# Transposing attention probabilities by row halves, at another place in the order of the engines

## The reference

```python
xn = layernorm(x)                                  # x: 8 batches, 256 rows, 128 columns, float32
q  = rope(xn @ wq.T);  latent = xn @ w_kv_down.T   # 16 heads of 64; latent of 64
k  = rope(latent @ w_k_up.T);  v = latent @ w_v_up.T
s  = softmax(q @ k.T / 8 + causal) @ v @ wo.T      # per batch and head
g  = silu(2 * expert_of_each_row(xn))              # 8 experts, gelu, 128 -> 512 -> 128
out = x + s * g
```

## Time and profile before

| what | value |
|---|---|
| median of 3 runs | 302.62 us (302.54 to 303.06) |
| the profiled execution, its own time | 303.29 us |
| its span | 301.5 us |
| PE busy | 289.6 us (96%) |
| ACT, DVE, POOL busy | 239.3, 229.7, 213.5 us |
| granted TensorE clock | 1.0 of full speed throughout |

### The profile page before, as it was taken

The page is one execution under the profiler, slowest core; times in us unless marked ns, Lnnn a source line. Parts: engine busy times, 40 slices in busy tenths (PEclk is TensorE's granted clock), DMA queues, the critical chain, the costliest instruction groups (busy, mean ns, idle before and its releaser), DMA issues.

```text
span 301.5 us, 8603 instructions
## 1 busy us (share of the span) xinstructions
PE 289.6 (96%) x2362; PEld 235.0 (78%) x2362; DVE 229.7 (76%) x909; ACT 239.3 (79%) x863; POOL 213.5 (71%) x325
## 2 busy tenths in 40 slices
PE   8798999999999999999999989999999999999994
PEld 2576888888888888777776779999977778887663
DVE  4889998987777898988898723444377889898981
ACT  4278789898887889989998676677787898999971
POOL 2478878697778669999999982333226899998730
PEclk9999999999999999999999999999999999999999
DMA  6864685879333233444333382000234243543410
GB/s 192 249 133 115 114 276 148 205 194 300 87 75 68 60 75 83 107 101 102 90 97 90 112 245 55 2 0 2 66 93 108 64 113 99 121 106 109 113 37 17
DMA packets 39596, 33.35 MB, mean 111 GB/s; under 512 B 4801, under 2 KB 36674, under 8 KB 39554
## 3 DMA queue, kind: packets, MB, share of 16 engines
q1 hardware_dynamic: 38098, 30.51, 39.8%
q0 software_dynamic: 1024, 2.10, 2.4%
q10 hardware_dynamic: 432, 0.23, 0.3%
HBM read 11.07 MB, written 4.98 MB: 53 GB/s over the span
## 4 chain that ended last, share of the span: by engine, by line
PE 64%; POOL 14%; DVE 9%; issue 6%; DMA 3%; ACT 1%; POOLq 0%; SPq 0%; DVEq 0%; ACTq 0%
PE bank L1199 9%; PE bank L1187 9%; PE bank L1216 8%; PE bank L1450 7%; PE bank L1438 6%; PE bank L1233 6%; POOL probs L499 5%; POOL staged L488 5%; PE bank L1161 3%; DVE rot_out L617 3%; PE bank L1218 3%; PE bank L1189 3%; POOL xn L515 3%; DMA qk_sb<-staged 3%; DVE masked L633 2%
## 5 line engine op out<-in xcount | busy, mean ns | idle before, releaser
L975 ACT ACTIVATE pexp<-masked,negmax 128x128 f32<-128x128 f32 (+1 forms) x256 | 113.9, 452 | 2.2 <-DVE negmax L633 2.2
L499 POOL TENSOR_SCALAR probs<-pexp,rden 128x128 f32<-128x128 f32 (+1 forms) x195 | 84.3, 447 | 27.0 <-DVE rden L640 25.2
L633 DVE CUSTOM_DVE_ANT_0 masked<-bank,mask 128x128 f32<-128x128 f32 (+1 forms) x256 | 75.9, 352 | 21.4 <-PE bank L1189 20.5
L488 POOL TENSOR_TENSOR staged<-rot_out 128x512 f32<-128x512 f32 x56 | 71.4, 1278 | 16.2 <-DVE rot_out L617 15.6
L617 DVE TENSOR_TENSOR rot_out<-bank,rot 128x1024 f32<-128x1024 f32 x64 | 77.7, 1215 | 4.6 <-PE bank L1163 3.5
L997 ACT COPY probsT<-bank 128x384 f32<-128x384 f32 x126 | 54.0, 480 | 27.3 <-PE bank L1199 26.0
L1199 PE MATMUL bank<-ident,probs 128*128 128x128 f32 x384 | 54.0, 275 | 0.7 <-issue 0.5
L975 ACT ACTIVATION_READ_ACCUMULATOR pexp<-masked,negmax 128x1 f32 x256 | 50.0, 195 | 0.0
L1187 PE MATMUL bank<-qk_sb 64*128 64x256 f32 x256 | 47.0, 428 | 1.7 <-DMA qk_sb<-staged 1.3
L1199 PEld LDWEIGHTS bank<-ident,probs 128*128 128x128 f32 x384 | 43.0, 140 | 3.4 <-issue 1.2
L1233 PE MATMUL bank<-vo_sb,ctxT 128*128 128x128 f32 x256 | 37.8, 278 | 0.7 <-ACT ctxT L1004 0.7
(11 more groups left out here) (117 smaller groups left out, 483.6 us busy)
## 6 DMA issues: line engine op xcount, KB each, us to landing
qk_sb<-staged SPq DMA_DIRECT2D x128, 128.0 KB
w_sb<-in_w SPq DMA_DIRECT2D x2, 1024.0 KB, 5.8
w_sb<-in_w SPq DMA_DIRECT2D x4, 512.0 KB, 5.3
sorted_x<-z SPq DMA_DIRECT2D x1, 1408.0 KB, 8.0
sorted_g<-z SPq DMA_DIRECT2D x1, 1152.0 KB, 5.5
out<-res SPq DMA_DIRECT2D x8, 128.0 KB, 2.3
x_sb<-in_x SPq DMA_DIRECT2D x3, 256.0 KB, 3.8
rot<-in_c_rot SPq DMA_DIRECT2D x1, 512.0 KB, 5.7
```

The source lines that it names most:

```text
L488: pool.tensor_tensor(staged[:, n % 2, :, m % 2, :], rot_out[:, m % 2, :, 0:S], rot_out[:, m % 2, :, S:2 * S], op=ALU.add).then_inc(staged_ ...
L499: pool.tensor_scalar(probs[:, g % 2, i, c], pexp[:, g % 2, i, c], rden[:, g % 2, i, k:k + 1], 1.0, ALU.mult, ALU.mult).then_inc(probs_read ...
L633: t = dve.tensor_tensor_reduce(masked[:, g % 2, i, c], s_bank[i][:, c], mask[:, c], -1.0, -NEG * 1e8, ALU.add, ALU.min, negmax[:, g % 2, i ...
L975: e = act.activation(pexp[:, g % 2, i, c], masked[:, g % 2, i, c], ACT.Exp, bias=negmax[:, g % 2, i, k:k + 1], scale=-1.0, accum_out=rowsu ...
```

## The change

In slots 2 to 35 and in the periods (units 43 to 56), a transposition is made from 64 rows at a time: for each piece of 128 columns there are two transpositions, one of the upper 64 rows of `probs` into `bank2` and one of the lower 64 rows into `bank3`. A unit has 12 of them, of 64 rows by 128 columns, where it had six of 128 by 128. Each bank then holds both heads' halves, and ACT's two copies write runs of 64 columns; both copies wait for all 12.

The place moves too. `TURN_LAST` names the slots 2 to 35 and the odd units 43 to 55. There turn(g) is PE's last work of the slot or period, directly ahead of the next scores, and ACT's copies stand one slot later in its list, between the two exponentials of that slot. For the even units 44 to 56 turn(s) keeps its place behind scores(s+3). Since the copies of the odd unit now come later, values of two units in a period is cut into one call part for each unit, each with its own wait.

```diff
+TURN_LAST = (*range(2, G_LEAD - 4), *range(PERIODS[0] + 1, PERIODS[-1], 2))
+HALVED = (*TURN_LAST, *PERIODS[1:])
...
+        def turned_half(g, i):
+
+            whole = probsT[:, g % 4].rearrange("p i (k q c) -> p (i k) q c", q=2, c=HD)
+            return whole[:, :, i, :]
...
+                if g in HALVED:
+                    act.wait_ge(probsT_done, 2 * g + 2)
+                    for i in range(2):
+                        act.copy(turned_half(g, i), t_bank[i][:, 0:SW].rearrange("p (n c) -> p n c", c=HD)
+                                 ).then_inc(probsT_ready, 1)
+                    return
...
+                if g - 1 in TURN_LAST:
+                    turned_probs(g - 1)
                 if more:
                     exponentials(g + 1, 1)
...
-                if g not in (G_LEAD, G_LEAD + 1, LATE):
+                if g not in (G_LEAD, G_LEAD + 1, LATE) and g not in TURN_LAST:
                     turned_probs(g)
...
             def turn(g):
 
+                if g in HALVED:
+                    wait(pe, probsT_ready, 2 * g)
+                    for i in range(2):
+                        for k in range(3):
+                            if k < 2:
+                                pe.wait_ge(probs_ready[i][k], g + 1)
+                            for o, r in zip(t_bank, half_rows):
+                                t = pe.transpose(o[:, (3 * i + k) * HD:(3 * i + k + 1) * HD],
+                                                 probs[r, g % 2, i, k * P:(k + 1) * P], ident[r, r])
+                        t.then_inc(probsT_done, 1)
+                    return
...
-                pe.wait_ge(probsT_ready, 2 * (g + n))
-                pairs = slice(g % 4, g % 4 + n)
...
+                parts = ((g, 1), (g + 1, 1)) if g in PERIODS and g + 1 in TURN_LAST else ((g, n),)
+                for j, k in parts:
+                    pe.wait_ge(probsT_ready, 2 * (j + k))
...
             # period(s)
-                turn(s + 1)
+                if s + 1 not in TURN_LAST:
+                    turn(s + 1)
                 for m in items(s + 1):
                     project(m)
                 for m in items(s)[1:]:
                     project(m)
+                if s + 1 in TURN_LAST:
+                    turn(s + 1)
...
             # slot(g)
-                else:
+                elif g not in TURN_LAST:
                     turn(g)
...
+                if g in TURN_LAST:
+                    turn(g)
                 for m in items(g)[1:]:
                     project(m)
```

More of the change, by code:

```diff
@@ L1211, in values @@
                     wait(pe, ctx_ready, values_through(min(g, LATE)) - 1)
-                pe.wait_ge(probsT_ready, 2 * (g + n))
-                pairs = slice(g % 4, g % 4 + n)
[L1214 to L1218, removed]
+                parts = ((g, 1), (g + 1, 1)) if g in PERIODS and g + 1 in TURN_LAST else ((g, n),)
+                for j, k in parts:
+                    pe.wait_ge(probsT_ready, 2 * (j + k))
+                    pairs = slice(j % 4, j % 4 + k)
+                    at = slice((j - g) * S, (j - g + k) * S)
+                    o = (w_bank if g == LATE else o_bank)[:, at].rearrange("p (n s) -> p n s", s=S)
+                    for i, r in enumerate(half_rows):
+                        pe.matmul(o[r, :, :], lat_all[:, 2 * b, :], probsT[:, pairs, i, 0:S], start=True, stop=False)
+                    for i, r in enumerate(half_rows):
+                        m = pe.matmul(o[r, :, P:S], lat_all[:, 2 * b + 1, :], probsT[:, pairs, i, S:SW],
+                                      start=False, stop=True)
                 m.then_inc(pv_done, 1)
```

## The result

The changed kernel takes 305.27 us (median of 7 runs, 304.05 to 306.26), the kernel before 303.05 on the same chip: ratio 1.0074, 95% interval 1.0052 to 1.0095. It is 0.7% slower, where 301.5 and a gain were forecast. The profiled execution took 305.54 us with a span of 303.1.

What follows compares the result with a forecast made beforehand. PE was taken as the bound, with DVE or POOL also full in some slots and a loop through ACT in the periods. Slots -4.7 and periods +3.6 gave -1.1: 301.5 us, own range 299 to 304, with rivals 296.5 to 306.5.

Steps and rivals of the forecast that it cites:

- The sum: Whole kernel: slots -4.7 and periods +3.6 us give -1.1, so 301.5 us for the median.
- the slots: Slots 2 to 35: PE's saving, as far as DVE and POOL leave room, shortens them by 4.7 us together.
- the periods: Seven periods: a longer loop through ACT adds 3.6 us, bounds +3.0 to +4.5.
- The transposition itself: PE, each unit: six pairs of halves at 0.060 us take 0.36 in place of 0.65, saving 0.29 us.
- I cost that at nothing: PE's tiling changes: their number stays, and one exposed load replaces another, 0.05 us either way, counted as no cost.
- Rival 1: PE's transpositions: a pair of halves is no faster than 0.11 us; 308.5 us in all, chance 0.12.
- The gain is what the fullest engine leaves: Slots 2 to 35: PE's 0.29 us a slot counts only as far as DVE or POOL has idle time.
- rival 3: Slots 2 to 20: late copies make PE wait, giving back all (306.2 us) or half (304.0) of the saving; chance 0.23.
- The loop in the periods: Periods: the chain from odd copies through PE and ACT to the next takes 7.41 us, 0.69 longer than 6.72.
- Rival 2: Periods: odd copies are not in the loop, only POOL bounds them, 1.6 us to gain; 296.3 us, chance 0.15.
- the entry: First periods: ACT's 1.26 us wait lets the first gain 0.4 us; the second ends 0.2 behind, five more add 0.69 each.
- the bounds -2.5 and +4.5: Least gain allowed for the early slots (-2.5 us) and greatest loss allowed for the late periods (+4.5 us).

Runs made afterwards that it cites:

- e10_stay: Against the kernel before: in the slots only, halved transpositions at their old place, with ACT's old list; 304.95 us against 302.81, ratio 1.0063.
- e3_whole: Against the kernel before: in the slots only, whole transpositions moved to the slot's end with the later copies; 306.04 us against 302.88, ratio 1.0102.
- e5_zero: Against the kernel before: the change in the slots alone, with the zero fill of sorted_x issued in slot 15, not 9; 299.97 us against 302.63, ratio 0.9916.
- e11_list: Against the kernel before: only the odd units' copies in the periods one slot later in ACT's list, values cut in two; 308.37 us against 302.81, ratio 1.0184.
- e2_periods: Against the kernel before: the change in the periods alone, slots 2 to 35 as before; 307.57 us against 302.88, ratio 1.0157.
- e12_after_zero: The whole change, with the zero fill of sorted_x issued in slot 15, not 9; 304.89 us against 302.73 for the kernel before, ratio 1.0077.
- e4_first: The whole change, but in the periods the odd unit's copies ahead of both heads' exponentials; 301.67 us against 302.88 for the kernel before, ratio 0.9957.
- e1_slots: Against the kernel before: the change in slots 2 to 35 alone, periods as before; 300.49 us against 302.88, ratio 0.9916.
- e9_both: The whole change on PE, ACT's old list in the periods, sorted_x's zero fill in slot 15; 298.39 us against 302.81 for the kernel before, ratio 0.9855.

## Why the prediction was wrong

The sum was -1.1 us and the change measured +2.2; +1.6 of it is in the span. Both terms of the sum missed, to the same side: the slots, put at -4.7, gave -2.9, and the periods, put at +3.6, gave +4.8.

**The transposition itself: right.** A pair was taken at 0.060 us, loads measured 0.06 and matmuls 0.07, and the unit saves 0.29 as forecast. "I cost that at nothing", said of the changes of tiling, holds too, but only for this neighbour: in e10_stay and e3_whole a change costs 0.09 to 0.16 us more, where halves stand amid whole rows or whole pieces ahead of scores. Rival 1 is refuted. It drew on the rule of the Trainium skill (TensorE: Matmul & The Clock Gate, LDWEIGHTS), columns / 1.2 ns. An estimate by that rule is 107 ns for a pair; it takes 60 to 70 here.

**The first step that failed: the size of the slots' gain.** "The gain is what the fullest engine leaves" is right as a mechanism, but I read what an engine leaves from sums over four slots. Slots 6 to 20 were costed at -4.0 (1.0, 1.1 and 1.9) and gave -1.9. The trace puts four waits of PE there, 0.43, 0.48, 0.80 and 0.41 us, 2.1 together, where it puts none before: 0.29 earlier a slot, PE comes ahead of DVE's rotations in single slots, and one late operand (0.80 us) takes back three slots' savings. e5_zero shows that one operand's cause. For the rotations no run was made. PE's waits for `probsT` in slots 6 to 20, which rival 3 needs, are not in the trace; it is refuted as a mechanism. POOL's rounds bound slots 24 to 35, as forecast.

**The loop in the periods: right.** 7.41 us was worked out, 7.40 measured, with PE idle 1.0 us ahead of the second part of values. PE's part of the chain, from the odd copies' end (231.34) to the even copies (233.57), is 2.23 where 2.30 stood, and ACT's, from there to 238.74, is 5.17 where 5.11 stood. So two small errors cancel; on PE scores took 0.76 where 0.65 stood. Rival 2 is refuted, by e11_list above all.

**The second step that failed: the entry.** "ACT waits 1.26 us before the first such copies (unit 43), so the first period is still PE's and gains 0.4; the second ends 0.2 behind". That 1.26 was no slack for the new order. In the old list the copies of unit 43 stood ahead of the scaling of unit 44, and the reciprocal for that scaling came late, behind a rotation and an addition on DVE. Timelines of DVE and ACT in the kernel before:

```profile
230.23 1.22 DVE L617 TENSOR_TENSOR rot_out<-bank,rot 128x1024 f32<-128x1024 f32 x1
...
232.09 0.17 DVE L640 RECIPROCAL rden<-rowsum 128x4 f32<-128x4 f32 x1
...
232.35 0.40 ACT L988 ACTIVATE probs<-pexp,rden 128x128 f32<-128x128 f32 x1 [0.19 <-issue]
```

The 1.26 of waiting and the copies' 0.86 covered it: the scaling itself waited only 0.19. In the new list the scaling, and one head's exponentials, stand ahead of the copies. ACT is idle for 2.31 us until that reciprocal (229.06), scales at 229.32 and copies at 230.51, and the loop is closed in the first period. Seven times 0.69 is 4.83, which is what the trace shows. e2_periods shows the same from its first period on, without an earlier start, and e11_list shows the same 2.31 us. My +3.6 gave the first two periods 1.2 us that they never had, and my upper bound of +4.5 left the case out.

**The balance.** The two sizes moved the sum across zero. Against a loop of which I was sure, -4.7 was the part with the weaker ground: from slot 6 to slot 20 it took nearly all that PE offered. I named the bounds -2.5 and +4.5 myself; their sum, +2.0, is nearly what happened. It gives 304.6, already above the 304 at which my own range ended, and the chance of a slower kernel there (0.06 of 0.50) was too small. The range 296.5 to 306.5 held the time, since it was wide enough for the rivals, and not because the forecast was near. The 0.6 us outside the span were in no term.

## What to carry to other kernels

A wait that an engine shows ahead of a step is slack only for the order it stands in: before spending it, ask what the waiting hid, and follow the steps that move ahead of it to their own last operand. What PE saves in a slot is worth what the engines and DMAs leave in that slot, not what they leave on average over several; a full sum of such savings is a bound. When a form and a place change together, cost each change of tiling at both neighbours: here either alone lost, and both together won.

## What the runs showed of the hardware

- Transpositions of 64 rows by 128 columns in the two halves of the rows run side by side: 0.06 to 0.07 us for a pair, where one of 128 rows takes 0.109. The page puts no idle time of PE ahead of any of the 576 (0.0 us), so issue of the 24 instructions for a unit did not hold the matmuls up.
- What a change of tiling costs depends on the neighbour (one slot of each trace): 0.09 more from project to halves than to whole transpositions, 0.10 more from output to values when halves stand ahead of output, and 0.16 more from whole transpositions to scores than to output.
- The time outside the span is not constant. In the kernel before it is 1.8 us in every execution whose span is on record. It is 1.8 to 2.8 in the seven of the changed kernel (2.4 in the profiled one), 2.3 to 2.9 in the six of e12_after_zero, 1.8 to 2.6 in those of e4_first, and 1.8 to 1.9 in e1_slots, e2_periods and e11_list. In e9_both it is 2.8 in the profiled execution with a span of 295.4, and 1.8 to 1.9 in the other three with 296.6, while the whole time is the same within 0.3. The last instructions look the same in these traces. What makes it was not tried. It is 0.6 us of the 2.2 measured.
